# The batch statistics of the second convolution product, taken one group earlier in the Vector engine's order

## The reference

```
agg = einsum('nm,bmd->bnd', A_hat, features);  x = agg.reshape(-1, 256)
h   = relu(batchnorm(x @ W1.T + b1, g1, be1))      # 512 columns
out = h @ W2.T + b2                                # 256 columns
out = batchnorm(out, g2, be2)                      # mean and variance over all 8192 rows
```

## Time and profile before

| | |
|---|---|
| median of 3 runs | 2142.96 us (2142.67 to 2145.03) |
| the profiled execution's own time | 2142.67 us |
| its span in the trace | 2140.9 us (1.8 us lie around it) |
| PE busy | 1994.8 us (93%) |
| DVE busy | 1273.1 us (59%) |
| ACT busy | 983.8 us (46%) |
| first and last matmul of `conv_second` start | 1845.37 and 1938.20 us |

### The profile page before, as it was taken

One profiled execution on the slowest core, in us unless ns is written; L12 is line 12 of the kernel. 1 busy time (PEld: TensorE's weight loads), 2 busy tenths in 40 slices (PEclk: granted clock), 3 DMA queues, 4 the chain that ended last, 5 costly groups with the idle time before them and its releaser, 6 DMA issues. The chain is left out here.

```text
span 2140.9 us, 33706 instructions
## 1 busy us (share of the span) xinstructions
PE 1994.8 (93%) x12342; PEld 1627.6 (76%) x12342; DVE 1273.1 (59%) x2675; ACT 983.8 (46%) x1659; POOL 223.4 (10%) x203
## 2 busy tenths in 40 slices
PE   7998999999999999999998799999998798895998
PEld 6997888888899999888886457566575676684887
DVE  7453665445445555555654666666753677884886
ACT  2544554333334343323322563645544244673885
POOL 1000000000011101010111530101100011100000
PEclk9999999999999999999999999999999899997999
DMA  3201001000100000001004221415140211001232
GB/s 114 78 2 40 0 0 40 0 0 0 39 1 0 0 0 14 17 1 79 0 0 147 89 89 46 131 46 160 60 150 1 89 59 49 12 0 50 80 105 82
DMA packets 83053, 100.05 MB, mean 47 GB/s; under 512 B 8976, under 2 KB 75152, under 8 KB 80656
## 3 DMA queue, kind: packets, MB, share of 16 engines
q1 hardware_dynamic: 82960, 98.79, 14.2%
HBM read 61.78 MB, written 33.55 MB: 45 GB/s over the span
## 5 line engine op out<-in xcount | busy, mean ns | idle before, releaser
L669 ACT ACTIVATE b_gate<-b_pG,b_bias 128x512 f32<-128x512 f32 (+1 forms) x504 | 304.3, 633 | 369.5 <-PE b_pG L54 368.6
L52 PE MATMUL b_pG<-b_xshi,b_whi 128*128 128x512 f32 (+1 forms) x1008 | 369.7, 367 | 6.3 <-DVE b_xslo L726 5.8
L54 PE MATMUL b_pG<-b_xshi,b_wlo 128*128 128x512 f32 (+1 forms) x1008 | 370.1, 367 | 0.0
L53 PE MATMUL b_pG<-b_xslo,b_whi 128*128 128x512 f32 (+1 forms) x1008 | 369.7, 367 | 0.0
L722 DVE CAST b_xshi<-HT 128x512 fp32r<-128x512 f32 (+3 forms) x144 | 59.7, 455 | 275.8 <-PE b_pG L54 275.7
L52 PEld LDWEIGHTS b_pG<-b_xshi,b_whi 128*128 128x128 f32 x1008 | 189.8, 188 | 36.0 <-DVE b_xslo L726 6.0
L53 PEld LDWEIGHTS b_pG<-b_xslo,b_whi 128*128 128x128 f32 x1008 | 189.8, 188 | 28.7
L54 PEld LDWEIGHTS b_pG<-b_xshi,b_wlo 128*128 128x128 f32 x1008 | 189.8, 188 | 27.7
L54 PE MATMUL b_pG<-b_hshi,b_wlo 128*128 128x512 f32 (+1 forms) x576 | 206.9, 359 | 0.0
L53 PE MATMUL b_pG<-b_hslo,b_whi 128*128 128x512 f32 (+1 forms) x576 | 206.2, 358 | 0.0
L52 PE MATMUL b_pG<-b_hshi,b_whi 128*128 128x512 f32 (+1 forms) x576 | 206.0, 358 | 0.0
(11 more groups left out here) (341 smaller groups left out, 3964.0 us busy)
## 6 DMA issues: line engine op xcount, KB each, us to landing
a_xt<-in_x SPq DMA_DIRECT2D x16, 512.0 KB, 6.1
h_scratch<-HT SPq DMA_DIRECT2D x4, 2048.0 KB, 7.6
l_x<-in_x SPq DMA_DIRECT2D x16, 512.0 KB, 3.9
l_w<-h_scratch SPq DMA_DIRECT2D x16, 512.0 KB, 5.1
x_scratch<-l_x SPq DMA_DIRECT2D x16, 512.0 KB, 3.3
c_x<-x_scratch SPq DMA_DIRECT2D x32, 256.0 KB, 3.6
x_scratch<-c_x SPq DMA_DIRECT2D x32, 256.0 KB, 2.7
l_x<-x_scratch SPq DMA_DIRECT2D x16, 512.0 KB, 3.9
```

The source lines that it names most:

```text
L52: nc.tensor.matmul(out, w_hi, x_hi, start=first, stop=False)
L53: nc.tensor.matmul(out, w_hi, x_lo, start=False, stop=False)
L54: return nc.tensor.matmul(out, w_lo, x_hi, start=False, stop=last)
L669: nc.scalar.activation(gate[s][:, g, 0:plan.n], pG[s][:, g, 0:plan.n], SIG[g], bias=bias[:, plan.p - 1, 2 * g + s:2 * g + s + 1])\
```

## The change

`measure` is called for the group of the same step, g, and no longer for g-1. It now also stands in step 0, and the call behind the last step is gone. There are still 16 calls with two `bn_stats` each; none is added or removed. The new parameter `b` isn't used in the function.

```diff
-                def measure(g):
+                def measure(g, b):
                     dve.wait_ge(sem["o_done"], g + 1)
                     for m in range(KD):
                         V.bn_stats(st2[:, m, g, :], H1g[:, m, g, :])
...
                         if isinstance(g, int) and g == NG - 2:
                             fold(1)
                             last_weights()
-                        if not (isinstance(g, int) and g == 0):
-                            measure(g - 1)
+                        measure(g, b)
                         if isinstance(g, int) and g == 1:
                             fold(0)
 
                 both_ends(dve, NI, body)
-                measure(NG - 1)
```

## The result

The changed kernel took 2155.76 us (median of 5 runs, 2155.12 to 2157.38), the kernel before 2144.63 us (median of 5, 2142.67 to 2145.53) on the same chip. The ratio is 1.0055, 95% interval 1.0040 to 1.0069: it is slower, by 11.1 us. A second set gave 2155.76 (4 runs) against 2145.30 (13 runs), ratio 1.0053, interval 1.0036 to 1.0070. One run of the kernel before, in the set beside the first four experiments, took 3298.5 us at a granted clock of 0.55; it is counted in the median given there (2144.24 us) and left out of the ratios.

A forecast was written before the change was run, and what follows sets the result against it. PE was taken to bound the stage, with little room on DVE. Start 3.23, steady 6.44 and end 0.10 gave 9.8 us, added to 2142.67 for 2152.4 us; range 2149.0 to 2155.5.

The forecast's parts named there:

- the steady loss: In conv_second from group 3 to 15: six pairs take 73.74 us instead of 67.30, 6.44 more.
- The chain `keep`, wake, statistics, split, next but one group: In conv_second's loop: 6.33 us from group g's end to g+2's start, 12.29 per two groups instead of 11.20.
- The late start of group 15: End of conv_second: group 15 itself starts late, costing 0.10 us.
- hidden: Rival for conv_second: the wait for keep fits the free room, every split in time, 2142.7 us; chance 0.06.
- every group pays: Rival for conv_second: ACT late too, each group loses 1.09 us, 6.5 more, 2158.9 us; chance 0.05.
- The clock's rival: Clock falls once in the gap before group 3, losing 1.7 us more, 2154.1 us; chance 0.22.
- The rival with the smaller loss: POOL's collisions off the path at conv_second's start: 1.29 instead of 3.23 us there, 2150.5 us; chance 0.14.
- I take 3.23, since both rows of before show the full price: Start of conv_second: group 3 late by 1.29 to 3.23 us, the latter with both POOL collisions on its split.
- the sum: Whole forecast loss: 3.23 at the start, 6.44 steady, 0.10 at the end, 9.8 us.
- `dense_attention` starts with the same order, shifted: Behind conv_second: the next stage keeps its order and only moves later; no cost charged.
- the rows of an idle stretch in layer 3: Clock evidence: after an idle stretch of 2.4 us (1978.7 to 1981.1) the granted clock stayed at 1.00.
- The base: Starting time for the forecast: the profiled execution's own 2142.67 us, the runs' median taken as only 0.3 higher.

The follow-up runs named there:

- the first four experiments: New order only in steps 0 and 1 (2148.90 us), only in the loop (2151.31); changed kernel with fold(0) in step 0 (2152.11), with keep signalling each piece (2152.59).
- loop_only: New order only in the loop (groups 2 to 13) and behind it, start as in the kernel before; 2151.31 us, ratio 1.0033.
- pieces: Changed kernel with keep signalling each of its two pieces and measure waiting for each; 2152.59 us, ratio 1.0038.
- the fillers: 57 filler matmuls in PE's idle stretches at the start of layer 3: in the kernel before 2142.54 us, in the changed kernel 2151.41 us.
- before_delayed: Kernel before with four chained unused memsets on DVE ahead of the stage's first bn_aggr, a pure delay; 2147.58 us, ratio 1.0014.

## Why the prediction was right or wrong

**Right: the mechanism and the steady loss.** The chain `keep`, wake, statistics, split, next but one group was predicted at 12.29 us per two groups and measured at 12.31 in the odd groups. The stage from group 3 to 15 lost 6.57 us for 6.44. `loop_only` and `pieces` show the pair and the wait as its cause. The late start of group 15 cost the 0.10 us that was taken: from its start to ACT's sight of its end it was 1949.24 - 1943.28 = 5.96 instead of 5.86.

**The rivals.** The wait was not hidden, and not every group pays. The clock's rival was not tested: it stood on a gap of 2.4 us ahead of group 3, the gap was 1.30, and the clock stayed at its upper level there. The rival with the smaller loss had 1.29 us for the start and the forecast 3.23; the 2.03 measured lies between them, with one collision on the path.

**Mis-sized: "I take 3.23, since both rows of before show the full price".** It was 2.03. The price of a collision with POOL falls on whoever comes second, which was POOL at the cast, and POOL's second operation ended beside a wait that the change itself had made. The prediction's own numbers had the cast at the fold's end and POOL 0.07 behind it, so POOL second; it charged both prices all the same. The cast's is 0.97 of the 1.20 us. In the rest, ACT's `keep(1)` ended 15.81 us after the first matmul instead of 15.96, since the clock rose 0.3 us earlier, and the cast began 0.59 behind the fold instead of 0.67. With this, the stage lost 8.7 us where the sum had 9.8.

**The step that failed: "`dense_attention` starts with the same order, shifted", costed at nothing.** The order was the same, but layer 3 took longer: 3.2 us in the profile. Of this, 2.2 us lie at its start, where the changed kernel's PE stood at the lower clock 1.1 us longer and fell back to it behind the fifth idle stretch; the rest lies in the last eight matmuls and is luck of the profiled execution of before. On the medians the excess over the stage's 8.7 is 2.4 us in the first set and 1.8 in the second. With the fillers the excess is 0.2. The intervals of the medians, some 3 us either way, don't exclude that it is nothing; that it is real rests on the profiles, where R was long in both of the changed kernel and the granted clock shows why. The prediction had looked for the clock's price inside the stage and used the rows of an idle stretch in layer 3 as evidence, without asking what a shift would do to that very stretch.

**The base.** The sum was put on the profiled execution's own 2142.67 us. That was the fastest of the five runs of before, one with the short R; medians of before were 2144.0 to 2145.3 in all four sets. So the miss of 3.3 us divides into 2.0 for the base and 2.4 for layer 3, less 1.1 that the stage had been overcharged. That this overcharge left the time only 0.3 us outside the range is luck. The range was also too narrow at its upper end: its bounds came from the stage alone.

Open is what decides whether R is long or short, what ties the stage's start to the clock, and why `before_delayed` met the long case in its profile but, by its median, seldom in the timed runs.

## What to carry to other kernels

Ahead of moving an instruction forward in an engine's queue, ask what it waits for and who stands behind it: here 1.2 us of statistics cost nothing as long as they asked for a result one group old, and 1.1 us per two groups when they asked for the newest. A stall that feeds the group after next is charged once per two groups, so follow the chain over the buffers before multiplying. And where a later stage starts with PE idle and at the lower clock, even a pure shift may move the end by a few us: put that into the range, and take the base from several runs.

## What was not expected of the hardware

- DVE's 128x2048 cast and subtraction and POOL's 128x512 operations exclude each other, and the first keeps its time: the cast took 2.19 us behind a POOL operation that had begun 0.18 us earlier, and 1.22 ahead of one that began 0.16 us later and then took 2.21 instead of 1.29. The Trainium skill ("GPSIMD Engine Reference", section "8. Key points") names the contention over shared interfaces; the trace agrees, and its rows show that it goes by who comes first.
- An idle stretch of PE of 2.37 us in layer 3 left the clock alone in some executions and was followed by a stretch at the lower level in others (0.54 over 3.7 us), with the same work around it.
- The statistics started 0.18 us behind ACT's end in the loop and 0.03 in the written-out steps. Where even groups set the pace, a pair took 12.38 us (`loop_only`), and 12.31 where odd ones did. The even group's wait on PE stands at the head of PE's loop; that this is the cause isn't shown.
